# A fused attention and feed-forward kernel: its written-out orders and its PSUM slots laid out anew

## What is computed

```
x = x + LN(attention(LN(x)))
x = x + LN(ffn(LN(x)))
# attention, 16 heads of 32: c_kv = x @ W_dkv + b; v = c_kv @ W_uv + b; c_q = x @ W_dq + b
#   q = rotary(c_q @ W_qr + b), k = rotary(x @ W_kr + b)
#   softmax(q k^T / sqrt(32)) v, then @ W_o + b_o
# ffn: h = fwht(x * SU_ug) / 64; up = h @ W_up.T * s, gate = h @ W_gate.T * s
#   fwht(silu(gate) * up * SU_dp) / 64 @ W_down.T * s
```

## Time and profile before

| | us |
|---|---|
| median of 3 runs | 1949.24 |
| lowest and highest | 1948.71, 1949.36 |
| the execution with the profile | 1946.86 |
| its span, first to last instruction | 1944.8 |
| PE busy in it | 1845.8 |
| DVE, ACT, POOL busy | 1263.3, 1159.8, 940.5 |

### The profile page before, as it was taken

The page is one execution under the profiler, slowest core; times in us unless marked ns, Lnnn a source line. Parts: engine busy times, 40 slices in busy tenths (PEclk is TensorE's granted clock), DMA queues, the critical chain, the costliest instruction groups (busy, mean ns, idle before and its releaser), DMA issues.

```text
span 1944.8 us, 45513 instructions
## 1 busy us (share of the span) xinstructions
PE 1845.8 (95%) x18248; PEld 1282.4 (66%) x18248; DVE 1263.3 (65%) x2477; ACT 1159.8 (60%) x2003; POOL 940.5 (48%) x990
## 2 busy tenths in 40 slices
PE   3689979999999999999999999999999999999998
PEld 1366545677767676777767776767677776766775
DVE  7877657676677656766677667765676667664322
ACT  3567989666556665566566655666556656664222
POOL 3625445554355455554465445545455446434422
PEclk9799999999999999999999999999999999999999
DMA  9735522464236445454346323543446434422422
GB/s 245 248 99 132 157 55 61 99 142 93 72 88 145 91 98 126 98 126 99 89 114 142 87 73 93 135 100 99 118 106 126 99 88 107 112 76 77 119 84 71
DMA packets 353009, 213.23 MB, mean 110 GB/s; under 512 B 285216, under 2 KB 286496, under 8 KB 351776
## 3 DMA queue, kind: packets, MB, share of 16 engines
q1 hardware_dynamic: 343536, 198.72, 42.1%
q10 hardware_dynamic: 9264, 11.61, 2.0%
HBM read 122.19 MB, written 20.98 MB: 74 GB/s over the span
## 4 chain that ended last, share of the span: by engine, by line
PE 73%; DVE 8%; ACT 6%; POOL 4%; issue 4%; DMA 3%; SPq 1%; POOLq 0%; ACTq 0%; DVEq 0%
PE ps L900 29%; PE ps L925 15%; PE ps L846 5%; PE ps L836 5%; PE ps L857 5%; PE ps L873 4%; PE ps L892 2%; PE ps L747 2%; PE ps L878 2%; DVE mx L1385 2%; PE ps L805 2%; ACT pr L1076 1%; POOL rs L1470 1%; DMA qT<-tok 1%; POOL pr L1496 1%
## 5 line engine op out<-in xcount | busy, mean ns | idle before, releaser
L1076 ACT ACTIVATE pr<-ps,exp_scale 128x512 f16<-128x512 f32 x512 | 352.0, 688 | 262.1 <-PE ps L857 252.9
L1496 POOL TENSOR_TENSOR pr<-p,pr 128x512 f16<-128x512 f32 x256 | 296.4, 1158 | 326.5 <-ACT p L1082 326.4
L1385 DVE TENSOR_REDUCE mx<-ps 128x1 f32<-128x512 f32 x512 | 333.2, 683 | 97.7 <-PE ps L846 95.6
L900 PE MATMUL ps<-x2T,gate_w 128*128 128x256 f16 x3072 | 377.5, 273 | 0.0
L900 PE MATMUL ps<-x2T,up_w 128*128 128x256 f16 x3072 | 377.2, 273 | 0.0
L925 PE MATMUL ps<-room 128*128 128x512 f16 x1536 | 363.4, 379 | 0.2
L1399 DVE TENSOR_TENSOR pr<-ps,pr 128x512 f16<-128x512 f32 x256 | 176.1, 688 | 257.8 <-ACT ps L1087 257.5
L900 PEld LDWEIGHTS ps<-x2T,gate_w 128*128 128x128 f16 x3072 | 298.1, 98 | 56.7 <-issue 4.4
L900 PEld LDWEIGHTS ps<-x2T,up_w 128*128 128x128 f16 x3072 | 300.2, 98 | 43.2
L1524 POOL TENSOR_TENSOR room<-room 128x256 f16<-128x256 f32 x256 | 170.9, 676 | 273.2 <-ACT room L1112 272.9
L925 PEld LDWEIGHTS ps<-room 128*128 128x128 f16 x1536 | 148.4, 98 | 158.3 <-POOL room L1524 6.2
(11 more groups left out here) (191 smaller groups left out, 2477.4 us busy)
## 6 DMA issues: line engine op xcount, KB each, us to landing
room<-down_mid SPq DMA_DIRECT2D x256, 256.0 KB, 3.0
xr<-in_x SPq DMA_DIRECT2D x34, 256.0 KB, 3.1
y_mid<-xr SPq DMA_DIRECT2D x32, 256.0 KB, 2.0
room<-y_mid ACTq DMA_DIRECT2D x32, 256.0 KB, 2.7
xa<-in_x SPq DMA_DIRECT2D x30, 256.0 KB, 3.9
out<-room SPq DMA_DIRECT2D x24, 256.0 KB, 3.3
x2T<-in_W_gate SPq DMA_DIRECT2D x5, 1024.0 KB, 5.8
gate_w<-in_W_down SPq DMA_DIRECT2D x4, 1024.0 KB, 7.5
```

The lines of the kernel that those rows point to most:

```text
L900: mm = nc.tensor.matmul(ffn_ps[i % 2][:, half * HALF:(half + 1) * HALF], weights[:, chunks[j // 4], kt, pw, j % 4 * P:(j % 4 + 1) * P], x2 ...
L1076: nc.scalar.activation(pr[:, p_buf(b, U), 0, 2 * j:2 * j + 2, :].rearrange("p h q -> p (h q)"), work[k], ACT.Exp, scale=exp_scale[:, 0:1]) ...
L1385: nc.vector.tensor_reduce(mx[:, t, h:h + 1], work[k], AX.X, ALU.max).then_inc(sm_freed.sem, 1)
L1496: nc.gpsimd.tensor_tensor(lo, p32[:], hi, ALU.subtract).then_inc(p_low.sem, 1)
```

## The change

The number of steps, the instructions in each, the buffers and the waits of each kind of step are the same. Rearranged are the five lists of `ORDER`, the five lists of `FRONT` and the two sets that choose PSUM slots. `ORDER` begins at another point of the same cycle: its pass now starts about 20 PE steps later (at `down.7@-1`), and those steps stand at the end of the pass, or of the front, instead. Beside that single steps and families trade places: in the front, SP issues two loads ahead of the first transposes, DVE takes `proj.2.1` ahead of `mtok.1` in the loop, and POOL has other steps between two `cut`s. The slots of 14 steps change. Some lines of the diff, of 397:

```diff
     PE="""
-        st.12@1 st.13@1 st.14@1 gate.3 up.3 down.0 st.15@1 st.16@1 down.1 gate.4 up.4 gate.5 up.5 st.17@1 av.6@1
...
+        smax.1.15@1 proj.2.1@1 av.4@1 av.5@1 gate.3 st.12@1 up.3 st.13@1 st.14@1 down.0 st.15@1 gate.4 up.4
...
     DVE="""
-        mtok.1@1 proj.2.1@1 low.6@1 gelu.2 gelu.3 low.7@1 low.8@1 gelu.4 gelu.5 low.9@1 norm.1@1 smax.2.0@1
...
+        smax.1.10@1 smax.1.11@1 smax.1.12@1 smax.1.13@1 gelu.1 fe.2@-1 smax.1.14@1 proj.2.1@1 fe.3@-1
+        smax.1.15@1 mtok.1@1 low.6@1 gelu.2 low.7@1
...
-MIDDLE = {('proj', 0, 0), ('proj', 2, 0), ('proj', 3, 1), ('smax', 0, 0), ('smax', 0, 11), ('smax', 0, 13),
...
+MIDDLE = {('proj', 0, 0), ('proj', 2, 0), ('proj', 3, 1), ('smax', 0, 0), ('smax', 0, 13), ('smax', 0, 4),
```

More of the change, by code:

```diff
@@ L86 @@
+        av.10@1 st.24@1 proj.3.0@1 down.5 down.6 smax.2.12@1 st.25@1 smax.2.13@1 gate.9 av.11@1 smax.2.14@1
+        smax.2.15@1 proj.3.1@1 st.26@1 up.9 st.27@1
     """,
     ACT="""
[L88 to L90 removed]
@@ L110 @@
[L110 to L119, removed]
@@ L125 @@
-        low.10@1 yn.3
+        gelu.3@-1 ys.3@-1 low.8 gelu.4@-1 low.9 norm.1 gelu.5@-1 yn.3@-1 low.10 smax.2.0 xs.0@1 gelu.6@-1
+        smax.2.1 smax.2.2 smax.2.3 smax.2.4 smax.2.5 smax.2.6 smax.2.7 smax.2.8 smax.2.9 smax.2.10 low.11
+        smax.2.11 xs.1@1 xn.0@1 low.12 proj.3.0 xn.1@1 gelu.7@-1 smax.2.12 gelu.8@-1 smax.2.13 smax.2.14
+        smax.2.15 mtok.2 norm.2 proj.3.1 low.13 low.14 gelu.9@-1 gelu.10@-1 xs.2@1 low.15 xn.2@1 low.16 xs.3@1
+        gelu.11@-1 low.17 gelu.12@-1 smax.3.0 smax.3.1 xn.3@1 norm.3 gelu.13@-1 low.18 smax.3.2 low.19
@@ new lines @@
+        gelu.14@-1 smax.3.3 smax.3.4 c.1@1 smax.3.5 smax.3.6 norm.4 c.0@1 smax.3.7 gelu.15@-1 smax.3.8 low.20
+        smax.3.9 smax.3.10 smax.3.11 fs.0@-1 low.21 proj.0.0@1 fe.0@-1 smax.3.12 smax.3.13 smax.3.14 smax.3.15
+        mtok.3 gelu.16@-1 proj.0.1@1 fs.1@-1 gelu.17@-1 low.22 low.23 fe.1@-1 low.24 gelu.18@-1 gelu.19@-1
+        norm.5 low.25 gelu.20@-1 smax.0.0@1 smax.0.1@1 smax.0.2@1 low.26 smax.0.3@1 smax.0.4@1 gelu.21@-1 low.27
+        gelu.22@-1 smax.0.5@1 smax.0.6@1 low.28 smax.0.7@1 smax.0.8@1 smax.0.9@1 gelu.23@-1 proj.1.0@1 low.29
@@ new lines @@
+        norm.6 smax.0.10@1 gelu.24@-1 low.30 low.31 proj.1.1@1 gelu.25@-1 smax.0.11@1 smax.0.12@1 smax.0.13@1
+        smax.0.14@1 smax.0.15@1 mtok.0@1 gelu.26@-1 norm.7 v.0@1 v.1@1 v.2@1 v.3@1 low.0@1 gelu.27@-1 o.0
+        low.1@1 gelu.28@-1 oe.0 smax.1.0@1 smax.1.1@1 smax.1.2@1 smax.1.3@1 ys.0 gelu.29@-1 yn.0 o.1 low.2@1
+        oe.1 low.3@1 smax.1.4@1 ys.1 smax.1.5@1 smax.1.6@1 smax.1.7@1 o.2 yn.1 oe.2 gelu.30@-1 gelu.31@-1
+        norm.0@1 ys.2 o.3 yn.2 proj.2.0@1 oe.3 low.4@1 fs.2@-1 smax.1.8@1 low.5@1 fs.3@-1 gelu.0 smax.1.9@1
@@ L194 @@
+        down.5 down.6 st.25@1 smax.2.12@1 smax.2.13@1 av.11@1 smax.2.14@1 gate.9 smax.2.15@1 proj.3.1@1 st.26@1
+        up.9 st.27@1
     """,
@@ L240 @@
-        low.0@1 norm.7 v.0@1 v.1@1 uhl.20 low.1@1 smax.1.0@1 o.0 oe.0 o.1 v.2@1 v.3@1 smax.1.1@1 smax.1.2@1
-        smax.1.3@1 uhl.21 uhl.22 oe.1 low.2@1 ys.0 smax.1.4@1 smax.1.5@1 yn.0 ys.1 uhl.23 low.3@1 uhl.24 o.2
-        oe.2 smax.1.6@1 uhl.25 uhl.26 o.3 uhl.27 yn.1 uhl.28 ys.2 uhl.29 oe.3 low.4@1 uhl.30 smax.1.7@1
-        smax.1.8@1 smax.1.9@1 uhl.31 smax.1.10@1 norm.0@1 smax.1.11@1 proj.2.0@1 low.5@1 yn.2 smax.1.12@1
-        smax.1.13@1 gelu.0 smax.1.14@1 smax.1.15@1 mtok.1@1 gelu.1 ys.3 proj.2.1@1 low.6@1 low.7@1 low.8@1
@@ L245 @@
-        gelu.2 gelu.3 low.9@1 gelu.4 low.10@1 gelu.5 smax.2.0@1 norm.1@1 yn.3
+        init xs.0 xs.1 xs.2 xs.3 xn.0 xn.1 xn.2 xn.3 amx.4 amx.3 amx.1 abias amx.2 amx.0 mx.0 adiag.0 asc amx.5
+        mx.1 adiag.1 mx.2 asd c.1 mx.3 hads arow mx.4 c.0 dmx proj.0.0 mx.5 brow proj.0.1 v.0 mx.6 dsc proj.1.0
+        v.1 mx.7 mx.8 proj.1.1 xs.0@1 smax.0.0 smax.0.1 smax.0.2 smax.0.3 smax.0.4 smax.0.5 smax.0.6 smax.0.7
+        smax.0.8 smax.0.9 smax.0.10 smax.0.11 smax.0.12 mx.9 smax.0.13 smax.0.14 smax.0.15 mtok.0 mx.10 dyl.0
@@ new lines @@
+        dyl.13 xs.3@1 norm.2 low.13 proj.3.1 smax.2.6 smax.2.7 smax.2.8 dyl.14 xn.3@1 smax.2.9 smax.2.10 dzl.8
+        dzl.9 dyl.15 low.14 smax.2.11 smax.2.12 smax.2.13 smax.2.14 smax.2.15 mtok.2 dzl.10 dzl.11 c.1@1 low.15
+        low.16 norm.3 dzl.12 low.17 dzl.13 c.0@1 dzl.14 low.18 low.19 smax.3.0 smax.3.1 smax.3.2 dzl.15 smax.3.3
+        smax.3.4 smax.3.5 smax.3.6 smax.3.7 smax.3.8 smax.3.9 low.20 smax.3.10 smax.3.11 norm.4 uhl.0 uhl.1
+        proj.0.0@1 low.21 smax.3.12 smax.3.13 uhl.2 uhl.3 low.22 low.23 smax.3.14 smax.3.15 mtok.3 uhl.4 uhl.5
@@ new lines @@
+        proj.0.1@1 uhl.6 uhl.7 low.24 norm.5 uhl.8 low.25 proj.1.0@1 uhl.9 uhl.10 uhl.11 low.26 low.27 uhl.12
+        smax.0.0@1 smax.0.1@1 smax.0.2@1 uhl.13 smax.0.3@1 smax.0.4@1 smax.0.5@1 uhl.14 proj.1.1@1 uhl.15 norm.6
+        uhl.16 low.28 low.29 smax.0.6@1 smax.0.7@1 low.30 smax.0.8@1 smax.0.9@1 smax.0.10@1 smax.0.11@1
+        smax.0.12@1 smax.0.13@1 smax.0.14@1 smax.0.15@1 mtok.0@1 uhl.17 uhl.18 low.31 norm.7 v.0@1 uhl.19 uhl.20
+        v.1@1 v.2@1 o.0 low.0@1 oe.0 smax.1.0@1 smax.1.1@1 smax.1.2@1 smax.1.3@1 low.1@1 uhl.21 ys.0 v.3@1 o.1
@@ L246 @@
+        yn.0 low.2@1 oe.1 o.2 smax.1.4@1 uhl.22 uhl.23 smax.1.5@1 smax.1.6@1 smax.1.7@1 low.3@1 ys.1 uhl.24 oe.2
+        uhl.25 ys.2 uhl.26 uhl.27 o.3 yn.1 low.4@1 uhl.28 uhl.29 norm.0@1 uhl.30 oe.3 yn.2 uhl.31 smax.1.8@1
+        smax.1.9@1 proj.2.0@1 smax.1.10@1 low.5@1 smax.1.11@1 smax.1.12@1 gelu.0 smax.1.13@1 gelu.1 smax.1.14@1
+        smax.1.15@1 mtok.1@1 proj.2.1@1 low.6@1 gelu.2 low.7@1
     """,
     POOL="""
-        xs.0 xs.1 xs.2 xs.3 xn.0 xn.1 xn.2 xn.3 asl.0 asl.1 asl.2 asl.3 asl.4 xs.0@1 asl.5 asl.6 asl.7 asl.8
@@ L254 @@
[L254 to L257 removed]
+        xs.0 xs.1 xs.2 xs.3 xn.0 xn.1 xn.2 xn.3 asl.0 asl.1 asl.2 asl.3 asl.4 asl.5 asl.6 asl.7 proj.0.0 tok.0.0
@@ new lines @@
+        asl.8 asl.9 proj.0.1 asl.10 asl.11 tok.0.1 proj.1.0 tok.1.0 cut.0 cut.1 cut.2 cut.3 proj.1.1 xs.0@1
+        tok.1.1 low.0 low.1 low.2 low.3 low.4 proj.2.0 cut.4 xn.0@1 tok.2.0 low.5 low.6 proj.2.1 norm.0 low.7
+        low.8 xs.1@1 tok.2.1 low.9 xs.2@1 xn.1@1 proj.3.0 low.10 tok.3.0 low.11 norm.1 xn.2@1 low.12 xs.3@1
+        low.13 xn.3@1 cut.5 proj.3.1 low.14 low.15 tok.3.1 norm.2 low.16 low.17 low.18 low.19 norm.3 cut.6
+        proj.0.0@1 low.20 low.21 low.22 low.23 tok.0.0@1 cut.7 proj.0.1@1 norm.4 cut.8 tok.0.1@1 low.24 low.25
@@ L258 @@
+        cut.9 low.26 low.27 proj.1.0@1 norm.5 tok.1.0@1 cut.10 low.28 low.29 low.30 norm.6 proj.1.1@1 low.31
+        tok.1.1@1 norm.7 cut.11 o.0 oe.0 low.0@1 low.1@1 ys.0 o.1 low.2@1 o.2 yn.0 oe.1 oe.2 ys.1 low.3@1 yn.1
+        low.4@1 ys.2 o.3 proj.2.0@1 low.5@1 tok.2.0@1 oe.3 yn.2 hid.0 low.6@1 norm.0@1 proj.2.1@1 hid.1 low.7@1
+        tok.2.1@1 hid.2 hid.3 low.8@1 low.9@1 ys.3 hid.4 low.10@1 hid.5 yn.3 norm.1@1
     """,
     SP="""
-        xl.0 xl.1 lda.4 lda.2 ldv.2 xl.2 xl.3 lda.3 lda.1 lda.5 ldx.0 ldv.0 lda.0 ldx.1 ln1.0 xl.0@1 ln1.1 ldx.2
```

280 lines of the change are left out of this document (129 added, 151 removed), and 9 rows, old and new, of tables (MIDDLE, UPPER).

## The result

The changed kernel takes 1966.03 us in the median of 4 runs (1965.06 to 1969.69), where before took 1949.3: a ratio of 1.0087 with an interval of 1.0075 to 1.0099. It is slower by 0.9%. The forecast was 1938.6, faster; the time lies outside the range, and even the slower rival (1955) is passed by 11 us. One of the ten runs of experiment 11 was slow (2054.7, at a lower granted clock) and is left out of its ratio.

The account below looks back on a forecast made before the run. PE was taken to bound the loop, other engines mattering only where PE waits. Terms +1.0 - 10.3 + 3.5 - 3.8 - 1.0 = -10.6 took the span from 1944.8 to 1934.2, median 1938.6 us; range 1926 to 1954.

Parts of the forecast that it names:

- the slower rival: Loop: queries come late because distances shrank and transposes land slowly, so scores of groups 0 and 3 wait; 1955, chance 0.16.
- The three waits of the loop: PE's waits at group 1's last two maxima and st.14 go: 1.7 us a pass, six passes, -10.3 us.
- Place three: Loop: mtok.3 moves beside POOL's fe and low half, delaying gelu.16 and PE's gate.18; +3.5 us (0 to +7).
- Place two: Front: mtok.3 held by one cut instead of two, shortening PE's wait before uh.7; -3.8 us (0 to -9.9).
- The start: Front: two loads ahead of the first transposes remove DVE's wait for weights; -1.0 us (-4.3 to +4.3).
- `av` runs: Five more runs of av steps overall, front 7 more and back 2 fewer, 0.2 us each; +1.0 us.
- Given back: The three loop waits go, but gate.18 waits 1.0 each batch and the front stays; 1947 to 1951, chance 0.21.

Follow-up runs that it names:

- experiment 11: Kernel before with three loop moves: DVE's fe.3 behind gelu.0, proj.2.1 ahead of mtok.1, POOL's yn.2 behind hid.0; 1946.9 us, ratio 0.9984.
- experiment 12: Kernel before with only DVE's fe.3 moved behind gelu.0 in the loop; 1938.4 us, ratio 0.9946.
- Experiment 4: Kernel before with one swap in DVE's loop list, proj.2.1 ahead of mtok.1; 1949.0 us, ratio 0.9999.
- experiment 9: Changed kernel with DVE's mtok.3 alone moved behind gelu.16 in the loop; 1960.8 us, ratio 1.0058.
- Experiments 2: Changed kernel with four loop moves: DVE's mtok.3 behind gelu.16; POOL's yn.0 behind oe.1, fe.3 behind low.6, tok.0.1 behind hid.16; 1952.4 us, ratio 1.0016.
- 7: Changed kernel with seven single-step moves in the loop, one on DVE and six on POOL; 1945.6 us, ratio 0.9981.
- 10: Changed kernel with POOL's yn.0 alone moved behind its oe.1 in the loop; 1967.3 us, ratio 1.0092.
- Experiment 5: Changed kernel with ACT's dzh.15 moved behind exp.39 and exq.19 in the front; 1967.4 us, ratio 1.0094.
- Experiment 6: Changed kernel with SP issuing the front's first transposes ahead of the two loads, and DVE's mx.8 behind the third maximum; 1964.2 us, ratio 1.0075.

## Why the prediction was wrong

**The three waits of the loop (-10.3).** Their cause and size were right (1.7 x 6 is 10.2, and 10.3 with the unrounded waits): experiment 12 takes 10.6 us out of the median and 1.54 out of the mean pass, 9.2 in six. But the step "`proj.2.1` stands ahead of `mtok.1`, so [...] the 0.97 goes" is false as a saving. It says that `mtok.1` is late next and that its scores "stand far behind", and no row was read for that. Experiment 4 prices it: 1.01 at `st.16` in place of 0.97 at `st.14`. In the changed kernel `mtok.1` is even held twice, and `st.16` and `gate.4` take 0.98 of the 1.7 back.

**Place three (+3.5, at most +7).** The mechanism was forecast at the right place, `gate.18` behind `mtok.3`, and undersized: 1.26 a pass where the bounds ended at 1.0. The bound took one held instruction from the nearest row. `mtok` has two, and the second starts when the first is released, which is when the next POOL instruction starts. Behind a POOL that has work queued both are held. The prediction had such a pair in its own rows, 1.85 and 4.02 beside two `cut`s, and the trace of before has one in every pass of the loop (835.83, shown above); it did not carry this over to the loop. Alone, the place is worth 0.9 a pass and 5.2 in the medians (experiment 9), more than the 3.5 but within the 7.

**What was not in the sum.** This is the step that failed most. `st.6` 1.18, `gate.20` 0.65, `av.16` and `av.17` 0.50, `down.16` 0.28: 2.6 a pass that no term speaks of. I priced three places of an edit of some 400 lines and took the others at nothing. Experiments 2, 7 and 10 take them away, or most of them, with moves of single steps on DVE and POOL. Between the forecast span (1934.2) and the measured one lie 30.7 us. By the waits of the third pass, times six, 15.7 of them are here, 5.9 at `st.16` and `gate.4`, and 4.6 at place three; the rest is in the front and the back.

**Place two (-3.8).** Better than forecast at its place: `mtok.3` took 0.53 and 1.10 beside a low half and `tok`, no `cut` held it, and the idle before `uh` fell from 6.01 to 1.45. It was given back at 224.84, where ACT's `dzh.15` waits for a write with `exq.19` behind it. Experiment 5 shows no gain from removing part of this idle in turn, so what one wait of the front yields is in the main given back at the next. The forecast had counted on one `cut` beside `mtok.3`; that none stood there was not foreseen.

**The start (-1.0).** The first maxima came 6.2 us later and the last 2.3 later. Experiment 6 makes a cost likely, some 1.8 in the medians, so the loads do not seem to pay; it does not settle the sign. What the whole front costs can be bounded from all profiled executions. Counted from PE's first instruction to the first pass, with the 13.8 of the moved steps added to the old front, the four with the old front take 387.4 to 390.1 and the six with the new one 389.5 to 393.2. So the new front is some 3 us slower, and the 4.4 of the one pair of profiles holds part of the spread. The forecast for it was -3.4 (-3.8, -1.0 and seven `av` runs at +0.2).

**`av` runs (+1.0).** Seven more such runs in the front and two fewer in the back; no experiment isolates it.

**The rivals.** "Given back" had the right mechanism and 5.4 lost in place of 2.3 to 2.8 was beyond its bound. "Slower" had the wrong one: the transposes landed in 4.5 in the median (4.4 before; at most 7.5). `st.16` does wait for its queries, but since `mtok.1` is held, not since the landing is slow. The prediction leaned on the lock at one place only: the exclusive lock of the Trainium skill's page "SBUF — State Buffer", section "SBUF: two separate sides", was weighed for the front alone, as a reason why `mtok.3` could be held twice. Held twice is what the trace shows, in the loop (0.97 and 1.21) and in the front (0.53 and 1.10, though beside a low half and `tok` and not beside a `cut` and the sum); the rule should have been laid over every pair in the new lists.
